# Thirteen of sixteen sets with four images interleaved in one matmul stream, in a binarised 3x3 convolution

## The reference

```python
# x: 64 x 256 x 28 x 28;  M: 256 x 256 x 3 x 3;  Z: 8 x M's shape;  alpha: 256 x 1 x 1;  rv: 1 x 8
A   = m * m + sum(z * z, axis=0) / 100.0
inv = rsqrt(A)
w   = rv @ (z * inv) + m * inv
bw  = sign(w)
g   = (x - mean) / sqrt(var + 1e-5)          # mean and var of each image's 32 groups of 8 channels
ba  = sign(g)
out = conv3x3(ba, bw, padding=1) * alpha
return x + out
```

## Time and profile before

| | before |
|---|---|
| median of 3 runs | 479.79 us (479.0 to 480.05) |
| profiled execution | 480.06 us, span 478.3 us |
| busy: TensorE, VectorE, ScalarE, GpSimd | 451.8, 397.0, 326.1, 10.8 us |
| DMA | 124.55 MB, mean 260 GB/s |

### The profile page before, as it was taken

The page is one execution under the profiler, slowest core; times in us unless marked ns, Lnnn a source line. Parts: engine busy times, 40 slices in busy tenths (PEclk is TensorE's granted clock), DMA queues, the critical chain, the costliest instruction groups (busy, mean ns, idle before and its releaser), DMA issues.

```text
span 478.3 us, 8267 instructions
## 1 busy us (share of the span) xinstructions
PE 451.8 (94%) x2966; PEld 424.5 (89%) x2966; DVE 397.0 (83%) x781; ACT 326.1 (68%) x564; POOL 10.8 (2%) x55
## 2 busy tenths in 40 slices
PE   3778898999999999999999999999999999999994
PEld 1333467999999999999999999999999999999994
DVE  2468687899989898989898989899898989898686
ACT  2556887785959494949494959586777768594420
POOL 3000000000000000000000000000000000000000
PEclk9979999999999999999999999999999999999998
DMA  7999999078777777777776776767766677632345
GB/s 268 399 394 391 392 356 393 13 259 325 259 259 253 252 268 271 269 271 269 264 274 222 270 263 253 252 235 275 257 259 254 250 252 252 250 120 117 134 182 223
DMA packets 46234, 124.55 MB, mean 260 GB/s; under 512 B 3696, under 2 KB 4208, under 8 KB 46192
## 3 DMA queue, kind: packets, MB, share of 16 engines
q1 hardware_dynamic: 45488, 123.21, 70.4%
q10 hardware_dynamic: 704, 0.81, 0.5%
HBM read 72.62 MB, written 51.38 MB: 259 GB/s over the span
## 4 chain that ended last, share of the span: by engine, by line
PE 80%; ACT 5%; SPq 4%; DVE 4%; DMA 3%; issue 2%; DVEq 0%; ACTq 0%
PE conv_ps L402 76%; SPq L283 4%; DMA x_sb<-in_L_conv_Z_dram 2%; ACT signs L550 2%; PE wt_ps L360 2%; PE conv_ps L340 1%; DVE low L856 1%; DVE whole L847 1%; DMA part<-in_L_conv_M_dram 1%; DVE x_sb L875 1%; ACT unread L531 1%; ACT unread L533 1%; ACT whole L498 1%; SPq L286 1%; PE conv_ps L347 1%
## 5 line engine op out<-in xcount | busy, mean ns | idle before, releaser
L402 PE MATMUL conv_ps<-signs,wts 128*128 128x378 f32 (+3 forms) x2304 | 403.9, 337 | 3.1 <-ACT part L564 2.2
L402 PEld LDWEIGHTS conv_ps<-signs,wts 128*128 128x128 f32 x2304 | 401.1, 189 | 6.3 <-ACT part L564 3.3
L550 ACT ACTIVATE signs<-x_sb,shift,rstd 128x784 fp32r<-128x784 f32 x128 | 133.7, 1099 | 21.3 <-DVE shift L833 21.3
L564 ACT ACTIVATE part<-conv_ps 128x392 int32<-128x392 f32 x128 | 62.4, 487 | 68.3 <-PE conv_ps L402 68.3
L847 DVE SCALAR_TENSOR_TENSOR whole<-conv_ps,part 128x392 int32<-128x392 f32 x128 | 72.2, 564 | 38.5 <-PE conv_ps L402 34.9
L856 DVE SCALAR_TENSOR_TENSOR low<-whole,conv_ps 128x392 f32<-128x392 int16 x128 | 71.9, 562 | 4.4
L777 DVE BATCH_NORM_STATS2 bn<-x_sb 128x6 f32<-128x392 f32 x138 | 70.6, 556 | 0.0
L875 DVE SCALAR_TENSOR_TENSOR x_sb<-whole,alpha_sb,x_sb 128x1568 f32<-128x1568 int16 (+1 forms) x38 | 60.6, 1594 | 0.8
L875 DVE SCALAR_TENSOR_TENSOR x_sb<-low,alpha_sb,x_sb 128x1568 f32<-128x1568 f32 (+1 forms) x38 | 60.4, 1588 | 0.0
L533 ACT ACTIVATE unread<-x_sb 128x784 bf16<-128x784 f32 x59 | 50.4, 854 | 0.0
L531 ACT ACTIVATE unread<-x_sb 128x784 bf16<-128x784 f32 x59 | 50.2, 851 | 0.0
(11 more groups left out here) (56 smaller groups left out, 118.1 us busy)
## 6 DMA issues: line engine op xcount, KB each, us to landing
x_sb<-in_x_dram SPq DMA_DIRECT2D x64, 784.0 KB, 5.0
out_dram<-x_sb SPq DMA_DIRECT2D x62, 784.0 KB, 4.8
x_sb<-in_L_conv_Z_dram SPq DMA_DIRECT2D x64, 288.0 KB, 9.0
part<-in_L_conv_M_dram SPq DMA_DIRECT2D x8, 288.0 KB, 10.1
out_dram<-x_sb SPq DMA_DIRECT2D x1, 588.0 KB, 3.9
out_dram<-x_sb ACTq DMA_DIRECT2D x1, 588.0 KB, 4.5
out_dram<-x_sb SPq DMA_DIRECT2D x2, 98.0 KB, 3.2
out_dram<-x_sb ACTq DMA_DIRECT2D x2, 98.0 KB, 3.5
```

What stands on the lines that cost most here:

```text
L402: mm = pe.matmul(flat_tile(conv_ps[at][:, 0:COLUMNS], b, r0, r1, c0, c1), wts[:, ch, (down + 1) * KW + right + 1], e, start=n == 0, stop=n ...
L550: nc.scalar.activation(o, x_sb[:, slot_of(k * TRI + image), h], ACT.Sign, bias=shift[:, k % RING, image, h:h + 1], scale=rstd[:, k % RING, ...
L564: nc.scalar.activation(part[:, at, 0:COLUMNS], conv_ps[at][:, 0:COLUMNS], ACT.Copy, scale=-FRACTION / PACK, bias=FRACTION / 2).then_inc(pa ...
```

## The change

Sets 0, 1 and 15 stay in pairs (`paired`). In sets 2 to 14 the four images are interleaved pixel by pixel. A row of four images has 112 columns, a tile is 4 rows of all four images (448 columns), and a set has 7 tiles. `signs` has its channel half ahead of the pair, so that both pairs lie together.

`high_sum`, `low_sum` and `fraction` read PSUM with the view "p (f i) -> p i f": image by image, every fourth column, 112 for each image. So `part`, `whole` and `low` hold each image in a row, and the outputs (`output_fours`) read them in a row: 12 rows of four images at once (1344 elements), then the last 16 rows (1792 elements), each for two channel halves.

Signs of sets 2 to 14: of the eight half images, ScalarE writes the even ones into `signs` with a stride of four. The odd ones it writes in bf16 into a small buffer `flat` (two of them), and GpSimd copies them into `signs` with a stride of four. TensorE waits for both.

Transfers: an image of a changed set is stored in two parts (rows 0 to 11, rows 12 to 27), and its four loads are issued after the four second parts. The order of the first sets is changed: images 2 and 3 are in `ALONE` and image 4 is not, the first fractions come ahead of the sums and of the signs of the second pair, and the tiles of sets 0 and 1 are placed otherwise among the statistics.

```diff
-        ALONE = (0, 1, 4, 5, 9)
+        ALONE = (0, 1, 2, 3, 5, 9)
...
+        def paired(k):
+            return k < 2 or k == LAST_SET
+        def tiles_of(k):
+            return TILES if paired(k) else FOURS
...
+        def sums_of(k, at):
+            v = conv_ps[at][:, 0:columns(k)]
+            return v if paired(k) else v.rearrange("p (f i) -> p i f", i=TRI)
+        def kept_sums(v, k, b):
+            r0, r1 = row_span(k, b)
+            if paired(k):
+                return v[:, pair_of(b), r0 * ROW:r1 * ROW]
+            return v.rearrange("p q f -> p (q f)").rearrange("p (i f) -> p i f", i=TRI)[:, :, r0 * W:r1 * W]
...
             def half_signs(g, k, n):
+                    h, image = divmod(n, TRI)
+                    own, done = n % 2 == 0, signs_done if n % 2 == 0 else flat_done
+                    o = four_signs(k, n) if own else flat[:, n // 2 % 2]
...
+                if not paired(k):
+                    pool.wait_ge(rest_done, first_tile(k - 1))
+                    for n in range(1, HALVES * TRI, 2):
+                        pool.wait_ge(flat_done, pool_signs_ahead(k) + n // 2 + 1)
+                        nc.gpsimd.tensor_copy(four_signs(k, n), flat[:, n // 2 % 2]).then_inc(pool_signs_done, 1)
...
+            def output_fours(k, h, r0, r1):
+                slot = slot_of(k * TRI)
+                dve.wait_ge(low_done, first_tile(k) + r1 // FOUR_ROWS)
+                v = (whole if h == 1 else low)[:, k % 2].rearrange("p q f -> p (q f)")
+                v = (high(v) if h == 1 else v).rearrange("p (i f) -> p i f", i=TRI)[:, :, r0 * W:r1 * W]
+                o = x_sb[:, slot:slot + TRI, h, r0 * W:r1 * W]
+                nc.vector.scalar_tensor_tensor(out=o, in0=v, scalar=alpha_sb[:, h:h + 1], in1=o, op0=ALU.mult,
+                                               op1=ALU.add).then_inc(out_done, 1)
```

ScalarE, first set:

```diff
-            sums(2)
             fraction(0, 0)
-            sums(3)
-            fraction(1, 1)
+            fraction(0, 1)
+            sums(4)
+            fraction(0, 2)
             deviation(1, 0, PAIR, TRI)
-            half_signs(1, 0, 4)
-            half_signs(1, 0, 5)
-            fraction(2, 2)
-            half_signs(1, 0, 6)
-            half_signs(1, 0, 7)
-            fraction(3, 3)
+            for n in range(HALVES * PAIR, HALVES * TRI):
+                half_signs(1, 0, n)
+            fraction(0, 3)
```

ScalarE, sets 2 to 14:

```diff
+            for k in range(2, LAST_SET):
+                sums((k + 1) * TRI + 2)
+                sums((k + 1) * TRI + 3)
+                fraction(k, 0)
+                fraction(k, 1)
+                deviation(turn(k + 1), k + 1, 0, TRI)
+                set_signs(k + 1, 0, 2)
+                fraction(k, 2)
+                set_signs(k + 1, 2, 4)
+                fraction(k, 3)
+                set_signs(k + 1, 4, 6)
+                fraction(k, 4)
+                set_signs(k + 1, 6, 8)
+                sums((k + 2) * TRI)
+                fraction(k, 5)
+                sums((k + 2) * TRI + 1)
+                fraction(k, 6)
```

VectorE, sets 2 to 14:

```diff
+            for k in range(2, LAST_SET):
+                g = turn(k + 1)
+                image_stats((k + 1) * TRI + 2, lambda: tile_sums(k - 1, tiles_of(k - 1) - 2))
+                image_stats((k + 1) * TRI + 3)
+                group_steps(g, k + 1, (k + 2) * TRI)
+                tile_sums(k - 1, tiles_of(k - 1) - 1)
+                bounded(g, k + 1, 0, TRI)
+                negative_mean(g, k + 1, 0, TRI)
+                second_outputs(k - 1)
+                for b in range(TOP_PART // FOUR_ROWS):
+                    tile_sums(k, b)
+                output_fours(k, 1, 0, TOP_PART)
+                output_fours(k, 0, 0, TOP_PART)
+                tile_sums(k, 3)
+                image_stats((k + 2) * TRI, lambda: tile_sums(k, 4))
+                image_stats((k + 2) * TRI + 1)
```

278 lines of the change are left out of this document (164 added, 114 removed).

## The result

| | before | after |
|---|---|---|
| median of 4 runs | 479.92 us (479.0 to 480.35) | 484.86 us (483.9 to 485.81) |
| profiled execution | 480.06 us, span 478.3 us | 485.52 us, span 483.8 us |

What follows compares the result with a forecast made beforehand. The prediction took TensorE to bound the kernel, busy 94% of the span. From 480.1 us it took 6.5 for thirteen sets and 1.4 for the start, giving 472.2 (471.9 against the median), range 466 to 486.

Steps and rivals of the forecast that it cites:

- TensorE's set, 25.00 to 24.5 us: TensorE's matmuls, sets 2 to 14: 126 for 144, 0.50 us less a set, 6.5 us saved in 13 sets.
- cost grows with columns: Rival on TensorE: a matmul's cost grows with its columns, set 24.87 us, 477.0 us in all; chance 0.14.
- Strided reads free: VectorE and ScalarE reading every fourth PSUM column: no extra cost, tile sums 620 ns, fractions 534 ns.
- strided reads that cost: Rival on VectorE's PSUM reads: 498 us at half the upper price, 540 at the full price; chance 0.16.
- 4 x 0.65 more: ScalarE's signs: extra us a set if a stride of four costs twice per element on write.
- GpSimd's cast 0.95 us: GpSimd's four copies of 784 elements a set: 0.95 us each, three times that as upper end, hidden.
- The copy comes 2 us after shift, when the second output already runs: Argument against outputs waiting for GpSimd's copy of 1 us on the shared SBUF port.
- The round is 24.1 us, against 24.5 of TensorE. Fits by 0.4 us: Outputs, stores, loads, statistics, next outputs: fourth image 16 us after the outputs, then 8.1 us back.
- the walk through the queues: One set followed through ScalarE's and VectorE's queues at 3.5 us a tile: VectorE ends at 24.1, TensorE does not wait.
- The load round or the shared port decides: Rival on loads and outputs: round of 25.1 us gives 480 us, one us longer 493; chance 0.10.
- The start, 1.4 us: First sets' new order: 3.6 us won, 2.6 lost again, 0.4 of old idling added; net 1.4 us, maybe 0 to 3.6.
- the sum of 472.2: Forecast time of the whole kernel: profiled 480.1 us less 6.5 for the sets and 1.4 for the start.

Runs made afterwards that it cites:

- e8_small_loads: Changed kernel, but every load after the first 12 images fetches only 4 of 28 rows; stores, casts and order stay: 474.31 us, ratio 0.9884.
- e2_small_copy: Changed kernel, but GpSimd casts only 28 of 784 elements of each odd half image: 486.25 us, ratio 1.0138.
- e3_no_first_stores: Changed kernel without the stores of rows 0 to 11 of the images of sets 2 to 14: 482.79 us, ratio 1.0061.
- e7_no_pool: Changed kernel with ScalarE writing all eight half images with the stride of four and GpSimd copying nothing: 484.26 us, ratio 1.0086.

## Why the prediction was wrong

- **TensorE's set, 25.00 to 24.5 us: right.** 24.42 where nothing else waits. The 448-column form is 26 ns longer in duration than the 392 one was. The rival "cost grows with columns" (24.87) is out. The Trainium skill's 2.5 ns over the columns (TensorE: Matmul & The Clock Gate, "Back-to-back issue gap") gives 24.95 us as an estimate, 18 x 2.5 ns under 25.00. With 24.42 the trace doesn't agree for this kernel; the section itself calls the formula the gap of an isolated matmul and not of a stream with weight loads, which the prediction left out.
- **Strided reads free: right.** 613 and 621 ns, where 622 was forecast without a price for the stride. The rival that took 0.16 of the chances, strided reads that cost, is out.
- **ScalarE's signs: the upper bound was the value.** "4 x 0.65 more" was written as the end of a range; the row says 4 x 0.72 (1.82 us for 1.10). The Trainium skill's penalty for each new line of 16 bytes (SBUF — State Buffer, "Specifications (TRN2)") fits this write. It was costed as ScalarE's work, which has room, and not as a delay of the signs and fractions behind.
- **GpSimd's cast 0.95 us: wrong, 1.6 to 2.7** (within the upper end of three times as much). "The copy comes 2 us after shift, when the second output already runs" was right of the second outputs (2.08 us each; it is the cast that is held up there) and missed the first ones: 1.2 us more for `low`. It isn't what costs sets 3 to 13 their time (`e8_small_loads`, `e2_small_copy`).
- **The step that failed: "The round is 24.1 us, against 24.5 of TensorE. Fits by 0.4 us".** It was measured as 25.84 us in the round shown, against 24.42 of TensorE. Two things were left out. First, the sum of bytes had no first parts' stores, which share the queue with the loads: 6.4 MB for 5.05, at the forecast's own 360 GB/s 17.8 us for 14.0. That overstates the effect, since some 0.4 MB of them (1.1 us at 370 GB/s) pass after the fourth image has landed; the measured landing is 17.4 us for 16. Second, the sum followed only the fourth load, and the walk through the queues, which ends in "So TensorE does not wait", never places the first. It lands 10.2 us after the second outputs, behind four stores, about 22 us into the set, when ScalarE already waits for it with the fraction of tile 5 behind. In sets 3 to 13 the first of the two costs 4.8 us and the second 6.1; with the first parts' stores gone (`e3_no_first_stores`) only the second is left, and a round through it was 25.4 us.
- **The rival that named the place.** "The load round or the shared port decides" gave 480 for a round of 25.1; by its own rule of 13 us for one more microsecond, 25.4 gives some 484, where 484.86 was measured. That the two come out so close is in part luck, since it too had only the fourth load. It had a chance of 0.10. With a slack of 0.4 us on a sum whose largest term was an estimate, it should have had a good deal more.
- **The start, 1.4 us: wrong by 1.7.** Set 0 is as walked: TensorE runs on from 70.33, without a low clock, and set 1 begins 3.4 us earlier (3.6 forecast). Behind it the walk gave back 2.2 us; set 1 alone gives back 3.8 (28.8 us for 25.0). The start alone, with the old signs and the old order of set 1, gives back 1.9 and has its set 2 2.2 us earlier (118.45 for 120.68). The walk took signs at 1.1 us where half are 1.8. That this is the cause is likely and not shown by itself: with all eight signs strided (`e7_no_pool`) set 1 takes 30.6 us, with the old order of set 1 32.8.
- **Together:** 5.1 and 0.3 us lost where 6.5 and 1.4 were to be won are 13.3 us; the profiled execution, 485.52, is 13.3 above the sum of 472.2. With the loads cut, `e8_small_loads` (474.36 when profiled) is 2.2 us above it: its set 2 begins at 120.59 (1.7 late against the walk), and its sets 2 to 14 take 319.74 us (0.6 over 325.64 - 6.5, since set 2 still takes 26.7).

What stays open: why a set of the changed kernel waits at one of the two places, at both or at neither, so that sets vary between 24.4 and 26.7 us, and what exactly makes sets 1 and 2 long.

## What to carry to other kernels

Where a buffer's slots tie outputs, stores, loads and statistics into a loop, sum that loop for the first transfer and for the last one, with every transfer that is in the queue at the time, and compare it with the period of the bound engine. A margin of 2% on such a sum is none. When work is merged into larger pieces, what came in halves spread over a period comes at once, and the loop gets longer though the engine that was the bound gets cheaper. The cure was order: put the instruction that frees the slots ahead of those that only the next stage needs, and move whatever the delayed ones would hold up, or it costs more than it gives (476.87 us with both edits, 503.08 with one).

## What the runs showed of the hardware

- A write by ScalarE to SBUF with 16 bytes from element to element takes 1.82 us for 784 elements; 8 bytes took 1.10. A read of PSUM with the same distance cost nothing: 448 elements took 613 and 621 ns on VectorE and 532 on ScalarE, where 392 neighbours took 564, 562 and 487.
- GpSimd's casts and VectorE's outputs, which have two operands in SBUF, hold each other up, and the one that began first is not delayed. In the round after the one shown, the output at 310.20 us took its 2.08 and the cast that began behind it at 311.07 took 2.70. The output of `whole` at 315.88 took its 1.62; the cast that began behind it at 316.87 took 2.11, and the output of `low` that began behind that cast, at 317.41, took 2.80 for 1.61. An undisturbed cast of 784 elements took 1.6. This agrees with the Trainium skill (SBUF — State Buffer, "Who interferes with whom"), by which issue order decides who blocks.
- A matmul of 448 columns in one piece and those of 432 in four pieces make 193.8 ns in the mean of a set (24.42 us over 126).
- Stores issued behind loads on the same queue land late: 336 KB took 10.7 us (median) from issue, where 448 KB issued with no load under way took 4.1:

```profile
out_dram<-x_sb SPq DMA_DIRECT2D x52, 448.0 KB, 4.1
...
out_dram<-x_sb SPq DMA_DIRECT2D x52, 336.0 KB, 10.7
```
